# Start-up and one late wait of an AdaLN + FFN kernel: who scales batch b, in which order three engines cast, subtract and shift, and product order over four PSUM banks

## The chip, the cores and the metric

The kernel runs on one core of a Trainium2 chip. The metric is the device time of one execution in microseconds (us). The core has five engines that run side by side and meet at semaphores: TensorE (PE in the profile; its weight loads are PEld), VectorE (DVE), ScalarE (ACT), GpSimd (POOL) and SyncE (SP, which here issues every DMA). The matmul accumulators live in PSUM, eight banks of 128 x 512 f32, written `ps`.

## The reference, cut to what matters

```python
q_emb = relu(q @ W3 + b3)                 # [16, 1024], one row per batch
x1 = (n * v + v_sum) * q_emb[:, None, :]  # v: [16, 512, 1024], v_sum over the 512 tokens
y = relu(x1 @ W2 + b2)                    # first big product
gates = softmax(y @ W_router + b_router)  # 6 experts, the two best kept
out = x + y @ W_base + b_base + (y @ A_s) @ B_s + sum over experts of w_e * (y @ A_r[e]) @ B_r[e]
```

All of it is f32 with 1024 x 1024 weights.

## The kernel before, in words

Data is held transposed, features on the 128 partitions and the 512 tokens of a batch in the free dimension. Batches are taken in eight pairs (a, b). Each big product over a pair is a 2 x 2 block product done with seven block products in place of eight (a Strassen-Winograd scheme): `n` = 0 to 6 in the code, each 512 x 512 times 512 x 512. Quadrants of the input are G11, G21 (batch a, first and second half of the features) and G12, G22 (batch b), four tiles of 128 x 512 each, `k` = 0 to 3. Stage 1 (`pair(i)`, i = 0 to 7, g = i) makes y, stage 2 (`pair2(p)`, g = 8 + p) makes the output.

To keep f32 accuracy, every operand is split in a high part (a rounding copy to the type fp32r: `act_hi`, `w_hi`, `yhi`) and a low part (operand minus high part: `act_lo`, `w_lo`, `buf1_lo`), and every block product is three matmuls (`three`, L1372 to L1374). A group (`group(g, n, j)`) is one output tile: 4 values of k times 3 matmuls of 128 x 512. A product is four groups, 48 matmuls.

Each engine has its order written out by hand:

- ACT: sums of x over tokens (`x_sum`, L570), the scaling that makes x1 (`x_scale`, L578), high parts of activations (`high`, L610) and of y (`y_high`, L629), copies out of PSUM (`copy_p0` L637, `copy_u2` L645, `copy_u4` L653, `c12` L663).
- DVE: low parts of activations (`low`, L923), of weights (`w2_low`, L909) and of y (`y_low`, L1004), differences of quadrants (`t1` L935, `t2` L947, `t3` L956, `t4` L962), sums out of PSUM (`c11`, `c22`, `c21`, L969), and in the first pair weight sums `s12`, `s2` (L1094), `r12` for n = 4 (L1121), `r21` for n = 5 (L1133), and the scaling of G12 for pair 0 (L1097 and L1101, semaphores `late_sum`, `late_mean`, `late_x1`).
- POOL: in the first pair high parts of weights (`w2_high`, L524), `a_hi` and `a_lo` (L540, L542), four subtractions for n = 6 (L556), and for every quadrant the tiny product `shift` = token sum times q (`shift_of`, L519), for which `x_scale` on ACT waits.
- PE: the products in order; `project_y(i, c, j)` after the groups of n = 4, 5, 6 (and of the next n = 0) multiplies tile j of y by the router and adapter weights `a_hi`, `a_lo`. It needs that tile's low part. C11 and C12 are the first-half tiles of y of batch a and b.
- SP: all loads and stores, in one queue.

In pair i, DVE makes the low part of C12 tile 0 before `low(i, 6, 0)`, and those of tiles 1 to 3 inside the loop over `low(i, 6, j)`. `group(0, 0, j)` and `group(0, 1, j)` of the first pair loop over j outside and k inside. Before `group(8, 2, 0)` PE waits for `low_done`, which DVE gives when it has made `low_lo` (L1310).

Of the kernel before, what the change touches and what calls it, by code (L numbers as in the profile page):

```python
# [27 lines left out]
H = 4  # L28
# [9 lines left out]
def adaln_ffn(nc, xT, condT, w3, b3, w2, b2, wbase, bbase, acat, bcat, brouter, outT, E, R):  # L38
# [15 lines left out]
    with ExitStack() as ctx:  # L54
# [119 lines left out]
        w2_hi_done = sem("w2_hi_done")  # L174
        w2_lo_done = sem("w2_lo_done")
# [96 lines left out]
        def source_no(i, q):  # L272

            return (G21, G22).index(q) if i == 0 else 2 + 4 * (i - 1) + (G12, G22, G11, G21).index(q)
# [229 lines left out]
        def _(pool):  # L504
# [38 lines left out]
            for k in range(H):  # L543
                pool.wait_ge(s4_made, H)
                pool.wait_ge(w2_lo_done, 2 * H + k + 1)
                w2_high(4, r12, k)
            for k in range(H):
                pool.wait_ge(s3_made, H)
                w2_high(5, r21, k)
            for k in range(H):  # L550
                pool.wait_ge(w2_lo_done, 4 * H + k + 1)
                w2_high(6, r22, k)
            shift_of(1, G12)
            for k in range(H):
                pool.wait_ge(w2_hi_done, 5 * H + k + 1)
# [10 lines left out]
        def _(act):  # L566
            def x_sum(i, q, k, done=x_summed):
# [3 lines left out]
                                     accum_out=vsum[:, t:t + 1]).then_inc(done, 1)  # L571
# [131 lines left out]
            for k in range(H):  # L703
                x_sum(0, G12, k, late_sum)
# [23 lines left out]
            def pair(i):  # L728
# [160 lines left out]
        def _(dve):  # L889
# [177 lines left out]
            first_w2_low(0)  # L1067
            first_w2_low(1)
# [539 lines left out]
```

## Time and profile before

| | |
|---|---|
| median of 3 runs | 1469.94 us (1467.17 to 1470.19) |
| profiled execution, its own time | 1470.98 us |
| span of the profile | 1469.2 us |
| PE busy | 1434.4 us, 98% |
| DVE busy | 908.0 us, 62% |
| ACT busy | 673.7 us, 46% |
| POOL busy | 48.4 us, 3% |
| mean granted TensorE clock | 0.994 |

The span runs from the first to the last instruction of the profiled execution; the own time is 1.8 us longer and holds what lies around it. Busy time of an engine is not bound to be on the path: what matters is where PE, busy 98% of the span, waits. All times in rows are us from the span's start unless a column says ns.

### The profile page before, as it was taken

Reading aid. Unit: us, or ns where it says so; the run is one execution under the profiler, and the core shown is the slowest. Engines: PE = TensorE matmul, PEld = TensorE weight load, DVE = VectorE, ACT = ScalarE, POOL = GpSimd, SP = SyncE. Lnnn points to the kernel's source line nnn. Section 1 sums busy time; section 2 is a strip of 40 time slices with the busy share of each in tenths; the row PEclk is TensorE's granted clock in tenths of the full one; section 3 lists DMA queues with packets and bytes.
Section 4 is the critical chain, followed back from the end, with each engine's and each line's share of the span. In section 5 each row is a group of like instructions: output and inputs, shape, how many; then the busy total and the mean of one; then the engine's idle time right before and its main releaser. Section 6 shows DMA issues by size and latency. Waiting matters only on the chain.

```text
span 1469.2 us, 18249 instructions
## 1 busy us (share of the span) xinstructions
PE 1434.4 (98%) x6314; PEld 1171.1 (80%) x6314; DVE 908.0 (62%) x1545; ACT 673.7 (46%) x1295; POOL 48.4 (3%) x74
## 2 busy tenths in 40 slices
PE   8879999999999999999999999999999999999999
PEld 4668878788787887878887888888888888888887
DVE  6947566465664656646787856466564655555564
ACT  5565674756748567484543423131232323223230
POOL 3430000000000000000000000000000000000000
PEclk9999999999999999999999999999999999999999
DMA  8231332413324132242562815426172451726342
GB/s 302 78 116 51 119 111 74 134 58 118 105 79 137 53 127 94 80 136 86 208 237 76 283 59 199 166 86 245 65 257 81 165 200 51 273 65 212 132 130 100
DMA packets 107229, 196.30 MB, mean 134 GB/s; under 512 B 12160, under 2 KB 12160, under 8 KB 107136
## 3 DMA queue, kind: packets, MB, share of 16 engines
q1 hardware_dynamic: 107136, 195.13, 39.2%
q8 instruction: 50, 0.82, 0.2%
q14 instruction: 43, 0.35, 0.1%
HBM read 123.78 MB, written 71.30 MB: 133 GB/s over the span
## 4 chain that ended last, share of the span: by engine, by line
PE 90%; DVE 3%; issue 2%; ACT 2%; POOL 1%; DMA 0%; SPq 0%; ACTq 0%; DVEq 0%; POOLq 0%
PE ps L1372 30%; PE ps L1374 29%; PE ps L1373 29%; ACT src L578 1%; POOL w_hi L524 1%; ACT act_hi L610 1%; DVE w_lo L909 1%; DVE act_lo L923 1%; PE ps L1486 0%; DVE buf_lo L1004 0%; DMA src<-in_xT 0%; DVE buf L969 0%; PE ps L1480 0%; ACT src L570 0%; ACT yhi L629 0%
## 5 line engine op out<-in xcount | busy, mean ns | idle before, releaser
L1372 PE MATMUL ps<-act_hi,w_hi 128*128 128x512 f32 x1792 | 703.9, 393 | 9.4 <-DVE act_lo L923 7.6
L1373 PE MATMUL ps<-act_lo,w_hi 128*128 128x512 f32 x1792 | 699.8, 390 | 0.0
L1374 PE MATMUL ps<-act_hi,w_lo 128*128 128x512 f32 x1792 | 699.6, 390 | 0.0
L1372 PEld LDWEIGHTS ps<-act_hi,w_hi 128*128 128x128 f32 x1792 | 337.7, 188 | 81.2 <-issue 7.7
L1374 PEld LDWEIGHTS ps<-act_hi,w_lo 128*128 128x128 f32 x1792 | 337.9, 189 | 71.0
L1373 PEld LDWEIGHTS ps<-act_lo,w_hi 128*128 128x128 f32 x1792 | 338.0, 189 | 69.3
L610 ACT ACTIVATE act_hi<-src 128x512 fp32r<-128x512 f32 x380 | 233.5, 623 | 258.9 <-PE ps L1374 257.2
L923 DVE TENSOR_TENSOR act_lo<-src,act_hi 128x512 fp32r<-128x512 f32 x320 | 218.8, 688 | 154.7 <-ACT act_hi L610 153.7
L969 DVE SCALAR_TENSOR_TENSOR buf<-ps,bb_sb,buf 128x512 f32<-128x512 f32 x128 | 95.7, 749 | 165.2 <-PE ps L1374 148.1
L969 DVE SCALAR_TENSOR_TENSOR buf<-ps,b_sb,buf 128x512 f32<-128x512 f32 x96 | 71.7, 749 | 75.6 <-PE ps L1374 75.2
L629 ACT ACTIVATE yhi<-buf 128x512 fp32r<-128x512 f32 x128 | 80.0, 625 | 52.5 <-PE ps L1374 52.3
L645 ACT ACTIVATE buf<-ps 128x512 f32<-128x512 f32 x64 | 38.3, 598 | 126.7 <-PE ps L1374 126.7
L637 ACT ACTIVATE buf<-ps 128x512 f32<-128x512 f32 x64 | 37.9, 597 | 125.1 <-PE ps L1374 125.1
L578 ACT ACTIVATE src<-src,shift,qn 128x512 f32<-128x512 f32 x120 | 87.7, 803 | 11.7 <-POOL shift L519 11.7
L570 ACT ACTIVATE src<-src 128x512 f32<-128x512 f32 x124 | 76.8, 620 | 0.0
L653 ACT ACTIVATE buf<-ps 128x512 f32<-128x512 f32 x64 | 38.3, 598 | 80.1 <-PE ps L1374 80.1
L923 DVE TENSOR_TENSOR act_lo<-buf,act_hi 128x512 fp32r<-128x512 f32 x64 | 42.6, 687 | 49.6 <-ACT act_hi L610 49.6
L1372 PE MATMUL ps<-yhi,a_hi 128*128 128x512 f32 x128 | 51.1, 399 | 18.5 <-DVE buf_lo L1004 18.0
L920 DVE SCALAR_TENSOR_TENSOR act_lo<-src,act_hi 128x512 fp32r<-128x512 f32 x64 | 44.0, 687 | 34.7 <-ACT act_hi L610 34.7
L1004 DVE TENSOR_TENSOR buf_lo<-buf,yhi 128x512 fp32r<-128x512 f32 x64 | 43.8, 685 | 22.2 <-ACT yhi L629 22.2
L1373 PE MATMUL ps<-buf_lo,a_hi 128*128 128x512 f32 x128 | 50.1, 391 | 0.0
L1374 PE MATMUL ps<-yhi,a_lo 128*128 128x512 f32 x128 | 50.1, 391 | 0.0
(114 smaller groups left out, 1009.4 us busy)
## 6 DMA issues: line engine op xcount, KB each, us to landing
src<-in_xT SPq DMA_DIRECT2D x224, 256.0 KB, 2.8
y_scratch<-buf SPq DMA_DIRECT2D x128, 256.0 KB, 2.1
src<-y_scratch SPq DMA_DIRECT2D x128, 256.0 KB, 4.8
outT<-buf SPq DMA_DIRECT2D x128, 256.0 KB, 4.1
buf<-in_xT SPq DMA_DIRECT2D x32, 256.0 KB, 4.5
wl_raw<-in_wbase SPq DMA_DIRECT2D x6, 1024.0 KB, 6.2
r<-in_w SPq DMA_DIRECT2D x16, 256.0 KB, 8.0
wh_raw<-in_wbase SPq DMA_DIRECT2D x3, 1024.0 KB, 7.7
```

The lines of the kernel that those rows point to most:

```text
L570: nc.scalar.activation(src[:, t, :], src[:, t, :], ACT.Copy, accum_out=vsum[:, t:t + 1]).then_inc(done, 1)
L578: nc.scalar.activation(src[:, t, :], src[:, t, :], ACT.Identity, bias=shift[:, t:t + 1], scale=qn[:, H * HALF_OF[q] + k, 2 * i + BATCH_OF[ ...
L610: nc.scalar.activation(act_hi[:, slot(g, n, k), :], source[:, t, :], func).then_inc(hi_done, 1)
L629: nc.scalar.activation(yhi[:, (y_no(i, c, j) - 1) % 2, :], buf[:, j, :], func).then_inc(yhi_done, 1)
L645: nc.scalar.activation(buf2[:, j, :], ps[:, j, :], ACT.Copy).then_inc(u2_copied, 1)
L920: nc.vector.scalar_tensor_tensor(act_lo[:, s, :], source, 0.0, act_hi[:, s, :].bitcast(F32), ALU.max, ALU.subtract).then_inc(lo_done, 1)
L923: nc.vector.tensor_tensor(act_lo[:, s, :], source, act_hi[:, s, :].bitcast(F32), ALU.subtract).then_inc(lo_done, 1)
L969: nc.vector.scalar_tensor_tensor(buf, ps[:, bank, :], bias, buf, ALU.add, ALU.add).then_inc(done, 1)
L1004: nc.vector.tensor_tensor(lo, y, hi, ALU.subtract).then_inc(ylo_done, 1)
L1372: nc.tensor.matmul(out, wh, a_h, start=start, stop=False, skip_group_check=onto)
L1373: nc.tensor.matmul(out, wh, a_l, start=False, stop=False, skip_group_check=onto)
L1374: return nc.tensor.matmul(out, wl, a_h, start=False, stop=stop, skip_group_check=onto)
```

## The change

Four things are done. (1) In pair 0, batch b's first half (G12) is scaled by ACT (`x_scale(0, G12)`) with a `shift` from POOL, where DVE did it with its own mean; the sources are renumbered. (2) On DVE, ACT and POOL of the first pair, weight and activation parts stand at other places: DVE interleaves `w2_low(2)` with `t1` and `low(0, 2)` with `t2`; POOL makes the high parts of `s12` only after `low(0, 2, 3)`; the high part of the n = 4 weights is cast by ACT in place of POOL; `shift_of(1, G12)` stands ahead of the casts for n = 6. (3) PE does products 0 and 1 of pair 0 with k outside and the four banks inside (`first_groups`). (4) In every pair of stage 1 `y_low(i, C12, 1)` stands ahead of `low(i, 6, 0)`; and PE's wait for `low_done` moves from ahead of `group(8, 2, 0)` to ahead of the low-rank matmuls behind it.

```diff
@@ gpsimd @@
             for k in range(H):
                 pool.wait_ge(s2_made, k + 1)
                 w2_high(2, s2, k)
+                if k == 1:
+                    shift_of(0, G12)
             shift_of(0, G22)
+            pool.wait_ge(q_sum, 1)
+            pool.wait_ge(lo_done, op_no(0, 2, H - 1))
             for k in range(H):
                 pool.wait_ge(s1_made, k + 1)
-                pool.wait_ge(q_sum, 1)
                 w2_high(3, s12, k)
...
             for k in range(H):
-                pool.wait_ge(s4_made, H)
-                pool.wait_ge(w2_lo_done, 2 * H + k + 1)
-                w2_high(4, r12, k)
-            for k in range(H):
                 pool.wait_ge(s3_made, H)
                 w2_high(5, r21, k)
+            shift_of(1, G12)
             for k in range(H):
                 pool.wait_ge(w2_lo_done, 4 * H + k + 1)
                 w2_high(6, r22, k)
-            shift_of(1, G12)
@@ scalar @@
-            for k in range(H):
+            for k in range(H - 1):
                 first_hi(k)
             act.wait_ge(q_sum, 2)
             nc.scalar.activation(qrow[:, D // 2:D], ps[0:NB, Q_BANK + 1, :], ACT.Copy).then_inc(q_copied, 1)
+            first_hi(H - 1)
...
-            x_scale(0, G22)
             for j in range(H):
                 copy_p0(0, j)
+            x_scale(0, G12)
+            x_scale(0, G22)
...
                 if i > 0:
                     exponent(i - 1, GA)
+                else:
+                    for k in range(H):
+                        act.wait_ge(s4_made, H)
+                        act.wait_ge(w2_lo_done, 2 * H + k + 1)
+                        nc.scalar.activation(w_hi[:, 4, k, :], r12[:, k, :], ACT.Copy).then_inc(s4_hi_done, 1)
                 copy_u2(i, H - 1)
@@ vector @@
-            dve.wait_ge(late_sum, H)
-            nc.vector.tensor_scalar(shift[:, cols], vsum[:, cols], 1.0 / T, None, ALU.mult).then_inc(late_mean, 1)
-            dve.wait_ge(late_mean, 1)
-            for k in range(H):
-                t = tile(G12, k)
-                nc.vector.tensor_scalar(src[:, t, :], src[:, t, :], shift[:, t:t + 1], qn[:, k, 1:2],
-                                        ALU.add, ALU.mult).then_inc(late_x1, 1)
+            w2_low(2, s2, (0, 1))
             for k in range(H):
                 t1(0, k)
-            w2_low(2, s2)
+                if k >= 2:
+                    w2_low(2, s2, (k,))
             for k in range(H):
                 t2(0, k)
+                if k > 0:
+                    low(0, 2, k - 1)
+            low(0, 2, H - 1)
...
                 y_low(i, C12, 0)
+                y_low(i, C12, 1)
                 for j in range(H):
                     low(i, 6, j)
                     if j > 0:
                         c22(i, j - 1)
+                    if j >= 2:
                         y_low(i, C12, j)
@@ tensor @@
+            def first_groups(n):
+                for k in range(H):
+                    pe.wait_ge(lo_done, op_no(0, n, k))
+                    pe.wait_ge(w2_lo_done, H * n + k + 1)
+                    for j in range(H):
...
+                    if k == 0 and n == 0:
+                        turn(1)
...
             def low_rank_c11(p, j):
                 if j == 0:
+                    if p == 0:
+                        pe.wait_ge(low_done, 1)
                     pe.wait_ge(lr_lo_done, 3 * p + 1)
...
-                if p == 0:
-                    pe.wait_ge(low_done, 1)
```

On DVE, before, between the sum `s2` and the end of the n = 4 weight difference of the first pair (`src<-src` is `t1`, `buf<-src` is `t2`):

```order
L1094 TENSOR_TENSOR s<-s,r 128x512 x4
L1097 TENSOR_SCALAR shift<-vsum 128x4
L1101 TENSOR_SCALAR src<-src,shift,qn 128x512 x4
L935 TENSOR_TENSOR src<-src 128x512 x4
L909 TENSOR_TENSOR w_lo<-s,w_hi 128x512 x4
L947 TENSOR_TENSOR buf<-src 128x512 x4
L923 TENSOR_TENSOR act_lo<-buf,act_hi 128x512 x4
L969 SCALAR_TENSOR_TENSOR buf<-ps,b_sb,buf 128x512 x4
L909 TENSOR_TENSOR w_lo<-s,w_hi 128x512 x4
L1121 TENSOR_TENSOR r<-r,s 128x512 x4
```

The same stretch of DVE in the changed kernel, whose line numbers differ:

```order
L1101 TENSOR_TENSOR s<-s,r 128x512 x4
L916 TENSOR_TENSOR w_lo<-s,w_hi 128x512 x2
L941 TENSOR_TENSOR src<-src 128x512 x3
L916 TENSOR_TENSOR w_lo<-s,w_hi 128x512
...
L953 TENSOR_TENSOR buf<-src 128x512
L930 TENSOR_TENSOR act_lo<-buf,act_hi 128x512
L953 TENSOR_TENSOR buf<-src 128x512
L930 TENSOR_TENSOR act_lo<-buf,act_hi 128x512 x2
L975 SCALAR_TENSOR_TENSOR buf<-ps,b_sb,buf 128x512 x4
L916 TENSOR_TENSOR w_lo<-s,w_hi 128x512 x4
L1123 TENSOR_TENSOR r<-r,s 128x512 x4
```

The five scaling instructions are gone, and low parts stand between the differences; from `c11` (`buf<-ps,b_sb,buf`) on the order is as it was.

On POOL, before, from the casts of `s2` (n = 2) on, with the semaphores waited for:

```order
L524 CAST w_hi<-s 128x512 [waits s2_made] x4
L519 TENSOR_TENSOR shift<-vsum,q 128x4 [waits x_summed]
L524 CAST w_hi<-s 128x512 [waits q_sum,s1_made] x4
L540 CAST a_hi<-a_raw 128x1024 [waits a_loaded]
L542 TENSOR_TENSOR a_lo<-a_raw,a_hi 128x1024 [waits a_hi_made]
L524 CAST w_hi<-r 128x512 [waits w2_lo_done,s4_made] x4
L524 CAST w_hi<-r 128x512 [waits s3_made] x4
L524 CAST w_hi<-r 128x512 [waits w2_lo_done] x4
L519 TENSOR_TENSOR shift<-vsum,q 128x4 [waits x_summed]
```

And in the changed kernel:

```order
L522 CAST w_hi<-s 128x512 [waits s2_made] x2
L517 TENSOR_TENSOR shift<-vsum,q 128x4 [waits x_summed]
L522 CAST w_hi<-s 128x512 [waits s2_made] x2
L517 TENSOR_TENSOR shift<-vsum,q 128x4 [waits x_summed]
L522 CAST w_hi<-s 128x512 [waits s1_made,lo_done,q_sum]
L522 CAST w_hi<-s 128x512 [waits s1_made] x3
L541 CAST a_hi<-a_raw 128x1024 [waits a_loaded]
L543 TENSOR_TENSOR a_lo<-a_raw,a_hi 128x1024 [waits a_hi_made]
L522 CAST w_hi<-r 128x512 [waits s3_made] x4
L517 TENSOR_TENSOR shift<-vsum,q 128x4 [waits x_summed]
L522 CAST w_hi<-r 128x512 [waits w2_lo_done] x4
```

The casts of `s12` and the two `a` instructions now wait for `lo_done`, the four n = 4 casts are gone, and the last `shift` shown, that of (1, G12), has four casts less ahead of it.

## Rows read from the trace of the kernel before

**Rows 1.** The page, its first line.

```profile
span 1469.2 us, 18249 instructions
```

**Rows 2.** Waits of PE, whole span: us in total, times, longest us.

```profile
PE ps L1372 <- DVE buf_lo L1004: 18.0, 8, 6.0
PE ps L1372 <- DVE act_lo L923: 7.6, 2, 7.0
```

**Rows 3.** Timeline of PE: start, us, instruction, idle before and its releaser.

```profile
40.67 0.39 PE L1374 MATMUL ps<-act_hi,w_lo 128*128 128x512 f32 x1
48.05 0.77 PE L1372 MATMUL ps<-act_hi,w_hi 128*128 128x512 f32 x1 [6.99 <-DVE act_lo L923]
...
53.10 0.40 PE L1372 MATMUL ps<-act_hi,w_hi 128*128 128x512 f32 x1
...
61.27 0.39 PE L1372 MATMUL ps<-act_hi,w_hi 128*128 128x512 f32 x1
...
87.80 0.80 PE L1372 MATMUL ps<-yhi,a_hi 128*128 128x512 f32 x1 [5.96 <-DVE buf_lo L1004]
...
285.13 0.50 PE L1372 MATMUL ps<-yhi,a_hi 128*128 128x512 f32 x1 [1.73 <-DVE buf_lo L1004]
...
788.69 0.50 PE L1372 MATMUL ps<-act_hi,w_hi 128*128 128x512 f32 x1 [1.71 <-DVE low_lo L1310]
```

**Rows 4.** Windows: busy PE, PEld, DVE, ACT, POOL, then granted clock, DMA.

```profile
87.00:93.00 6.00, 5.21 (x12) 4.13 (x13) 3.51 (x6) 5.01 (x12) 0.20 (x1) 0.50 0.71 201
...
100.00:104.00 4.00, 2.29 (x10) 1.58 (x9) 3.56 (x7) 3.69 (x11) 0.00 (x0) 1.00 0.54 158
...
790.00:793.00 3.00, 3.00 (x9) 2.37 (x8) 3.00 (x6) 0.53 (x2) 0.00 (x0) 0.52 0.26 93
```

**Rows 5.** Timeline of DVE, first pair, up to product 2.

```profile
35.80 4.57 DVE L935 TENSOR_TENSOR src<-src 128x512 f32<-128x512 f32 x4
40.29 4.64 DVE L909 TENSOR_TENSOR w_lo<-s,w_hi 128x512 fp32r<-128x512 f32 x4
...
49.68 2.71 DVE L969 SCALAR_TENSOR_TENSOR buf<-ps,b_sb,buf 128x512 f32<-128x512 f32 x4
```

**Rows 6.** Timeline of DVE, first pair, low parts alone and beside POOL's casts.

```profile
57.13 2.48 DVE L923 TENSOR_TENSOR act_lo<-src,act_hi 128x512 fp32r<-128x512 f32 x4
...
75.37 4.11 DVE L909 TENSOR_TENSOR w_lo<-r,w_hi 128x512 fp32r<-128x512 f32 x4 [0.71 <-POOL w_hi L524]
```

**Rows 7.** Timeline of POOL, first pair.

```profile
38.33 1.50 POOL L540 CAST a_hi<-a_raw 128x1024 fp32r<-128x1024 f32 x1
39.90 2.68 POOL L542 TENSOR_TENSOR a_lo<-a_raw,a_hi 128x1024 fp32r<-128x1024 f32 x1
...
57.27 7.64 POOL L524 CAST w_hi<-r 128x512 fp32r<-128x512 f32 x1 [14.69 <-DVE r L1121]
...
74.72 6.35 POOL L524 CAST w_hi<-r 128x512 fp32r<-128x512 f32 x8 [7.23 <-DVE r L1133]
```

**Rows 8.** Timeline of ACT, first pair: scalings, and high part of C11 tile 2.

```profile
35.08 2.94 ACT L578 ACTIVATE src<-src,shift,qn 128x512 f32<-128x512 f32 x4 [2.09 <-POOL shift L519]
...
81.27 2.93 ACT L578 ACTIVATE src<-src,shift,qn 128x512 f32<-128x512 f32 x4 [8.32 <-POOL shift L519]
...
86.33 0.62 ACT L629 ACTIVATE yhi<-buf 128x512 fp32r<-128x512 f32 x1
```

**Rows 9.** A later pair: high part of C12 tile 1 (ACT), its store (SP).

```profile
277.99 0.62 ACT L629 ACTIVATE yhi<-buf 128x512 fp32r<-128x512 f32 x1
...
272.14 0.44 SPq L391 DMA_DIRECT2D y_scratch<-buf  x1
```

**Rows 10.** Timeline of DVE at the start of stage 2.

```profile
788.55 0.68 DVE L1240 TENSOR_TENSOR ha_lo<-ha_raw,ha_hi 128x512 fp32r<-128x512 f32 x1
...
796.11 0.68 DVE L1259 TENSOR_TENSOR buf<-ps,buf 128x512 f32<-128x512 f32 x1
```

**Rows 11.** The page, DMA issues: KB each, us to landing.

```profile
y_scratch<-buf SPq DMA_DIRECT2D x128, 256.0 KB, 2.1
```

More of the change, by code:

```diff
@@ L272, in source_no @@
         def source_no(i, q):
-            return (G21, G22).index(q) if i == 0 else 2 + 4 * (i - 1) + (G12, G22, G11, G21).index(q)
+            return (G21, G12, G22).index(q) if i == 0 else 3 + 4 * (i - 1) + (G12, G22, G11, G21).index(q)
         def tile_no(i, q, k):
@@ L566, in _, with x_sum @@
         def _(act):
-            def x_sum(i, q, k, done=x_summed):
+            def x_sum(i, q, k):
                 t = tile(q, k)
@@ L570, in x_sum @@
                 nc.scalar.activation(src[:, t, :], src[:, t, :], ACT.Copy,
-                                     accum_out=vsum[:, t:t + 1]).then_inc(done, 1)
+                                     accum_out=vsum[:, t:t + 1]).then_inc(x_summed, 1)
             def x_scale(i, q):
@@ L904, in first_w2_low, with w2_low @@
                                         ALU.subtract).then_inc(w2_lo_done, 1)
-            def w2_low(n, raw):
-                for k in range(H):
-                    dve.wait_ge(w2_hi_done, H * (n - 1) + k + 1)
+            def w2_low(n, raw, ks=range(H)):
+                for k in ks:
+                    if n == 4:
+                        dve.wait_ge(s4_hi_done, k + 1)
+                    else:
+                        dve.wait_ge(w2_hi_done, H * (1, 2, 3, 5).index(n) + k + 1)
                     nc.vector.tensor_tensor(w_lo[:, n, k, :], raw[:, k, :], w_hi[:, n, k, :].bitcast(F32),
@@ L1067, in _ @@
             first_w2_low(0)
+            condition(0)
             first_w2_low(1)
@@ L1083, in _ @@
             low(0, 0, 3)
+            w2_low(1, r12, (0,))
             condition(1)
-            w2_low(1, r12)
+            w2_low(1, r12, (1, 2, 3))
             for k in range(H):
@@ L1112, in first_pair @@
             def first_pair():
-                for j in range(H):
-                    low(0, 2, j)
                 for j in range(H):
@@ L1458, in group @@
                 mm.then_inc(bank_done, 1)
+            def first_groups(n):
[3 more added lines that the diff above has]
+                    for j in range(H):
+                        if k == 0:
+                            bank_free(0, n, j)
+                        cols = slice(j * P, (j + 1) * P)
+                        mm = three(ps[:, j if n == 0 else Z_BANK + j, :], w_hi[:, n, k, cols], w_lo[:, n, k, cols],
+                                   act_hi[:, slot(0, n, k), :], act_lo[:, slot(0, n, k), :], k == 0, k == H - 1)
+                        if k == H - 1:
+                            mm.then_inc(bank_done, 1)
+                    if k < H - 1:
+                        mm.then_inc(op_used, 1)
+                    if k == 0 and n == 0:
+                        turn(1)
             def project_y(i, c, j):
@@ L1489, in pair @@
             def pair(i):
-                for j in range(H):
-                    group(i, 0, j)
-                    if i > 0:
+                if i == 0:
+                    first_groups(0)
+                    first_groups(1)
+                else:
+                    for j in range(H):
+                        group(i, 0, j)
                         project_y(i - 1, C21, j)
@@ L1495, in pair @@
                             turn_h(i - 1, GB)
-                    elif j == 0:
-                        turn(1)
-                for j in range(H):
-                    group(i, 1, j)
-                    if j == 1 and i > 0:
-                        turn_gates(i - 1, GB)
+                    for j in range(H):
+                        group(i, 1, j)
+                        if j == 1:
+                            turn_gates(i - 1, GB)
                 for j in range(H):
```

20 lines of the change are left out of this document (7 added, 13 removed).

## The prediction, made blind

> **What bounds the kernel now.** The page's first line gives the span [rows 1]; the table before it says PE is busy for 98% of it. So the first view is who PE waits for [rows 2]: the low part of y on DVE (`buf_lo`, 18.0 us in 8 waits) and the low part of an activation (`act_lo`, 7.6 us). The timeline of PE places them [rows 3]. PE stands 6.99 us between products 1 and 2 of the first pair (until 48.05), 5.96 us in product 4 of the first pair ahead of `project_y(0, C11, 2)` (until 87.80), and 1.73 us in a later pair ahead of `project_y(i, C12, 1)` (285.13). The `buf_lo` total less 5.96 leaves 12.0 us in 7 such waits, one for each of the pairs 0 to 6. At the start of stage 2 it stands 1.71 us for `low_lo` (788.69). The rest is matmuls: 36 of them start between 53.10 and 61.27 [rows 3], 0.227 us each, so a product of 48 is 10.9 us and a `project_y` 0.7 us.
>
> Idle time also cost clock. From 87 to 93 the granted clock was 0.50, that is 1.2 in place of 2.4 GHz [rows 4], although PE was at work from 87.80: with the half us behind that window, about 3.0 us lost. The 12 matmuls from 48.05 to 53.10 took 5.05 in place of 2.7 us [rows 3], 2.3 lost. From 790 to 793 it was 0.52 [rows 4] after an idle of only 1.71 us, about 1.7 lost with the end of the stretch. After the like idle at about 101 it was 1.00 [rows 4].
>
> **The change, step by step.** My sum follows the DVE-ACT-POOL chain of the first pair, because PE waits for it.
>
> *Product 2 starts earlier.* Now ACT is free at 33.0 (35.08 less its wait of 2.09) and scales only G22 [rows 8]. In the new order four copies from PSUM come first (each about 0.5, an estimate by the pitch of 0.62 us instructions [rows 8]), less something under 1 us because the second half of q is turned after 12 matmuls of product 0 instead of after the whole first group with its wait. I take 34.2. Then eight scalings at 0.71 [rows 8] end at 39.9. DVE loses its scalings and finds its `t1` and `w2_low(2)` without a full port fight: they take 4.57 and 4.64 us for four now [rows 5] where four subtractions alone take 2.48 [rows 6]. Its first `low(0, 2)` then ends near 41, and with one `t2` and one `low` in turn (0.6 each) the last near 44.2; `c11` starts there and not at 49.68 [rows 5], 5.5 earlier. Product 1 now ends with the matmul at 40.67 [rows 3]; with k outside, products 0 and 1 no longer wait in between and end 1.4 earlier. PE then waits about 1.7 us, runs product 2 haltingly at first, and ends it near 53.2, 8 earlier than 61.27.
>
> *DVE up to the n = 5 weights.* Behind 44.2 DVE has the same work as before: 4 `c11` (2.64 by their pitch [rows 5]) and 34 subtractions at 0.60 [rows 6] up to the last `s3` (L1133), 20.5: end at 67.3 if nothing disturbs it. But the casts of `s12`, `a_hi` and `a_lo`, which POOL did at 35 to 42.6, now fall here, since the POOL order waits for `low(0, 2, 3)`. Their price: nothing at the least. At the most: POOL gets in only when DVE stops for the first cast (as the cast at 57.27, 7.64 us long [rows 7]), 0.5; three `w2_low(3)` beside casts at 1.03 and not 0.60 [rows 6], 1.3; one beside `a_hi`, 1.50 long, 0.9 more; one behind `a_lo`, 2.68 long [rows 7], 2.2 more; together 4.9. `a_lo` and `a_hi` are priced by their own rows, the casts may in part pass beside `c11`; I take 4.0. So `s3` ends at 71.3, where POOL now starts its casts at 74.72 [rows 7]. `low(0, 3, 0)` comes at about 56.2, so PE gets a new wait of some 3 us ahead of product 3 (53.2 to 56.2); the 8 us gained are back to 5.
>
> The Trainium skill, GPSIMD Engine Reference, Specifications, says that GpSimd contends for SBUF with those VectorE instructions that have two SBUF inputs or run in a two-port mode. `c11` has one input in PSUM, so by that rule the `s12` casts would be done beside `c11`, the price would be nearer 3.1 than 4.0, and the forecast 1447.1. No row here has POOL at work beside an L969.
>
> *The n = 4 casts on ACT* cost ACT four instructions of 0.6 [rows 8] and put its `copy_u2(0, 3)`, `high(0, 4, j)` and the sums of the next pair behind `s4_made`. They end near 58, and DVE asks for `low(0, 4, 0)` only near 65: hidden. POOL loses its 7.64 us cast; nobody waited long for it.
>
> *The shift of (1, G12).* Now it comes behind 8 casts, 6.35 us [rows 7], and ACT waits for it 8.32 us, to 81.27 [rows 8]; from there it is 6.5 us to the matmul at 87.80 [rows 3] through `y_high(0, C11, 2)` at 86.33 [rows 8]. With four casts ahead of it: 71.3 + 3.2 + 0.2 = 74.7, then 6.5, then 0.3 for POOL's remaining casts and subtractions, which now fall beside DVE's `y_low`: 81.6. That is 6.2 earlier than 87.80. PE has come there at 56.2 + 10.9 + 9.5 = 76.6, so it still stands 5.0 us. Clock: the idle of 5.96 cost 3.0, idles of 1.7 cost 0 and 1.7; for 5.0 I take 2.5, a gain of 0.5. The bounds are 0 and 3.0.
>
> *`y_low(i, C12, 1)`.* In a later pair its high part is there at 277.99 + 0.62 [rows 9], and the store of its buffer was issued at 272.14 [rows 9] and lands about 2.1 us later [rows 11]. DVE can make it at 278.7 to 279.4; PE asks for it at 285.13 - 1.73 = 283.4 [rows 3]. All seven waits go: 12.0. Behind it on DVE stands `low(i, 6, 0)`, whose high part comes later still, so nothing is held up. What is late next on PE: nothing within 4 us.
>
> *`low_done`.* PE goes on 1.71 us earlier; `low_rank_c11(0, 0)` then comes one group (2.7) after 788.69 - 1.71 = 787.0, at 789.7, and its `ha_lo` is ready at 788.55 + 0.68 = 789.2 [rows 10]. With the idle goes its clock loss of 1.7. The add of the low-rank part at 796.11 [rows 10] may hold the third of these groups by a few tenths: 3.2.
>
> Sum: 6.2 + 0.5 + 12.0 + 3.2 = 21.9. The profiled execution took 1470.98 (span 1469.2), so 1449.1; it lies 1.04 above the median of 1469.94, and I forecast the median: 1448.0.
>
> **Rivals.**
>
> 1. *The port costs little or the clock stays up.* Casts beside `c11`, `a_lo` starved and done in a pause: contention nearly 0 gives 4.0 more, a kept clock 2.5 more. For it: casts of four took POOL only 3.2 [rows 7]. Against it: four subtractions beside `a_lo` took 4.64 [rows 5] and not 2.48 [rows 6], and `y_high` needs it. 1441.5; both halves seldom together, 1444 is its middle.
> 2. *The first pair gains nothing.* The moved POOL work, cold clock and ACT's stop at `s4_made` add up to 6.7 on the chain, for example if a starved `a_lo` (as the cast at 57.27 [rows 7]) stops ACT at `y_high(0, C11, 0)` and with it `high(0, 4, 3)`, about 4 us, on top of 4.0. Then 12.0 + 3.2 alone are left: 1454.7.
> 3. *The waits move on, the kernel doesn't get faster.* PE would stop at the next `project_y` or at product 6 in each pair. `c22` and `y_high(i, C12, 2)` depend on PE's own groups and move with it; I see nothing. 1463 (first pair and stage 2 alone, less 3).
> 4. *Slower.* `y_low(i, C12, 1)` also waits for the store of its buffer, and now stands ahead of the `low(i, 6, j)`. If stores landed late, DVE would stand with all of product 6 behind it. It decides from where the landing costs PE more than 1.73 in each of 7 pairs plus the other 9.9 / 7 = 1.4, so from 283.4 - 0.7 + 3.1 = 285.8, 13.7 us after issue at 272.14, against 2.1 in [rows 11]. At 15 us: 1479.
>
> **How the numbers follow.** My case 0.62, rival 1 0.20, rival 2 0.12, rival 3 0.03, rival 4 0.02, no change at all 0.01. What a measurement of this kernel can tell from no change is 0.2%, 2.9 us. Faster: 0.97. The range for 8 in 10 takes in my case with its bounds, 1444.5 to 1452, and most of rivals 1 and 2: 1442 to 1455.
>
> **What would show it.** Right: PE's waits have no `buf_lo` of 1.7 in pairs 0 to 6; the wait ahead of product 2 is under 2.5; a wait of 1 to 4 us stands ahead of product 3 and one of 3 to 5.5 ahead of `project_y(0, C11, 2)`, which starts at 80 to 83; `low_lo` is gone from the waits, and the clock near 790 is 1.00. Wrong: `c11` of pair 0 later than 46, ACT's `y_high(0, C11, 0)` waiting for `a_lo`, or a new PE wait of over 1 us that comes again in each pair.

## The result, and the profile after

| | before | changed |
|---|---|---|
| median | 1470.07 us (4 runs, 1467.17 to 1470.79) | 1448.88 us (4 runs, 1448.59 to 1449.11) |
| ratio | | 0.9859, 95% interval 0.9842 to 0.9877 |
| profiled execution, its own time | 1470.98 us | 1448.76 us |
| mean granted TensorE clock | 0.994 | 0.996 |

The changed kernel is 21.2 us faster by the medians and 22.2 by the two profiled executions (the one of the kernel before lies 0.9 above its median); 1448.0 was forecast. The page of the changed kernel, its first line and its first busy row, beside [rows 1]:

```profile
span 1446.7 us, 18245 instructions
...
PE 1429.2 (99%) x6314; PEld 1168.9 (81%) x6314; DVE 905.4 (63%) x1540; ACT 677.9 (47%) x1303; POOL 39.7 (3%) x71
```

PE is busy 5.2 us less than before in a span that is 22.5 us shorter: most of what went was idle time. Its waits, whole span, where [rows 2] had 18.0 us in 8 and 7.6 us in 2:

```profile
PE ps L1376 <- DVE buf_lo L1010: 6.0, 1, 6.0
PE ps L1376 <- issue: 4.2, 2, 3.0
```

One wait for `buf_lo` of this kind is left, 6.0 us long; the seven of 1.73 are gone, and so is the one for `low_lo`. The `act_lo` row is gone too, but two waits of 4.2 us in all stand under "issue" (a wait for nothing that the profile shows). The timeline of PE places all three, against [rows 3]:

```profile
39.24 0.39 PE L1378 MATMUL ps<-act_hi,w_lo 128*128 128x512 f32 x1
...
42.63 0.47 PE L1376 MATMUL ps<-act_hi,w_hi 128*128 128x512 f32 x1 [2.99 <-issue]
...
56.79 0.47 PE L1376 MATMUL ps<-act_hi,w_hi 128*128 128x512 f32 x1 [1.24 <-issue]
...
83.49 0.79 PE L1376 MATMUL ps<-yhi,a_hi 128*128 128x512 f32 x1 [6.01 <-DVE buf_lo L1010]
...
87.50 0.39 PE L1376 MATMUL ps<-act_hi,w_hi 128*128 128x512 f32 x1
```

PE stops after the matmul of 39.24, which ends product 1, and product 2 starts at 42.63; product 3 starts at 56.79, and `project_y(0, C11, 2)` at 83.49, 4.31 earlier than the 87.80 of [rows 3]. Whom the two "issue" waits were for is told by the timeline of DVE:

```profile
41.83 0.69 DVE L930 TENSOR_TENSOR act_lo<-buf,act_hi 128x512 fp32r<-128x512 f32 x1 [0.34 <-ACT act_hi L607]
...
45.64 2.72 DVE L975 SCALAR_TENSOR_TENSOR buf<-ps,b_sb,buf 128x512 f32<-128x512 f32 x4
...
48.27 5.41 DVE L916 TENSOR_TENSOR w_lo<-s,w_hi 128x512 fp32r<-128x512 f32 x4
...
56.01 2.48 DVE L930 TENSOR_TENSOR act_lo<-src,act_hi 128x512 fp32r<-128x512 f32 x4
...
81.68 1.75 DVE L1010 TENSOR_TENSOR buf_lo<-buf,yhi 128x512 fp32r<-128x512 f32 x1
```

The `low` at 41.83 ends at 42.52 and PE starts at 42.63; the first of the four at 56.01 ends 0.69 later, at 56.70, and PE starts at 56.79. Both waits are for low parts of an activation. `c11` (L975) starts at 45.64, not at 49.68 [rows 5]. And the `y_low` (L1010) that PE waits for at 83.49 took 1.75 us, where one alone takes 0.69. POOL says why:

```profile
45.84 2.29 POOL L522 CAST w_hi<-s 128x512 fp32r<-128x512 f32 x4 [10.56 <-issue]
48.08 1.04 POOL L541 CAST a_hi<-a_raw 128x1024 fp32r<-128x1024 f32 x1
49.20 2.72 POOL L543 TENSOR_TENSOR a_lo<-a_raw,a_hi 128x1024 fp32r<-128x1024 f32 x1
71.81 3.20 POOL L522 CAST w_hi<-r 128x512 fp32r<-128x512 f32 x4 [19.88 <-DVE r L1135]
74.97 0.64 POOL L517 TENSOR_TENSOR shift<-vsum,q 128x4 f32<-128x4 f32 x1
...
78.27 6.31 POOL L553 TENSOR_TENSOR w_lo<-r,w_hi 128x512 fp32r<-128x512 f32 x4
```

The casts of `s12` (45.84), `a_hi` and `a_lo` lie behind product 2's low parts, as the new order wants. The casts for n = 5 start at 71.81 and not at 74.72 [rows 7], and the shift of (1, G12) is done at 75.61. From 78.27 the four subtractions for n = 6 (L553) run, and `y_low` at 81.68 falls among them. ACT, beside [rows 8]:

```profile
30.94 0.63 ACT L567 ACTIVATE src<-src 128x512 f32<-128x512 f32 x1 [1.10 <-DMA src<-in_xT]
...
35.52 5.76 ACT L575 ACTIVATE src<-src,shift,qn 128x512 f32<-128x512 f32 x8
...
75.64 2.93 ACT L575 ACTIVATE src<-src,shift,qn 128x512 f32<-128x512 f32 x4 [7.05 <-POOL shift L517]
...
80.70 0.62 ACT L626 ACTIVATE yhi<-buf 128x512 fp32r<-128x512 f32 x1
```

ACT waited 1.10 us for a load of x at 30.94, began to scale G12 at 35.52, and scaled (1, G12) from 75.64, 5.63 earlier than 81.27 in [rows 8]. The high part of C11 tile 2 (80.70) is ready at 81.32. The granted clock, beside [rows 4]:

```profile
83.50:86.50 3.00, 3.00 (x7) 2.42 (x8) 2.83 (x3) 2.42 (x8) 1.08 (x1) 0.50 0.49 159
767.00:770.00 3.00, 3.00 (x16) 2.40 (x16) 2.64 (x5) 0.00 (x0) 0.00 (x0) 1.00 0.00 0
```

Behind the wait of 6.01 it is 0.50, as before; the stretch is shorter. The nine matmuls from 83.49 to 87.50 took 4.01 us, and 2.04 at the 0.227 of full clock: 1.97 lost. In the kernel before, the 14 matmuls from 87.80 to 93.89 (the first at full pitch again) took 6.09 in place of 3.18: 2.9 lost, behind a wait of the same length (5.96). At the start of stage 2 (767 to 770) the clock is 1.00.

**Where the time came from.** I subtract the start of the same matmul in one trace from that in the other, place by place. Product 2 starts 5.42 earlier, product 3 4.49 earlier, `project_y(0, C11, 2)` 4.31 earlier, and the matmuls behind both slow stretches of product 4 (from 93.89 before, 88.65 now) 5.24 earlier. Each of the pairs 0 to 6 then adds 2.01 to 2.06, 14.2 together. The start of stage 2 adds 3.1: 1.8 of wait and 1.6 of clock, less 0.3 that is given back further on, at 777.43, where PE now waits for DVE's add of the low-rank part. 5.2 + 14.2 + 3.1 = 22.5, the difference of the spans.

Of the 5.2, the last 0.9 is clock, and no run shows that the change made it: the wait in product 4 did not get shorter (6.01 and 5.96). Experiments 1 and 2 below keep the first pair of the kernel before, wait 5.74 and 5.59 there, and lose 1.6 and 1.7 behind it where the kernel before lost 2.9. The window of experiment 2 that stands beside the first of [rows 4], where the clock was 0.50:

```profile
87.00:93.00 6.00, 5.03 (x15) 4.05 (x16) 3.69 (x6) 5.17 (x13) 0.20 (x1) 0.64 0.74 208
```

So what the slow clock costs behind this wait differs by over 1 us between traces of the same first pair, and the first pair's gain is known no better than that: 4.3 at the start of `project_y(0, C11, 2)`, 5.2 behind it.

### The profile page after: what moved, and what is told of

Same layout as the page of the kernel before. It is cut to its first block, busy times and chain, and to the rows that moved or that the text cites. A ratio compares the mean times of both kernels' runs of the same rounds, so it can differ in the third digit from the quotient of the medians.

```text
span 1446.7 us, 18245 instructions
## 1 busy us (share of the span) xinstructions
PE 1429.2 (99%) x6314; PEld 1168.9 (81%) x6314; DVE 905.4 (63%) x1540; ACT 677.9 (47%) x1303; POOL 39.7 (3%) x71
## 4 chain that ended last, share of the span: by engine, by line
PE 93%; DVE 3%; ACT 1%; issue 0%; POOL 0%; DVEq 0%; ACTq 0%
PE ps L1376 31%; PE ps L1378 31%; PE ps L1377 31%; DVE act_lo L930 1%; PE ps L1508 0%; DVE w_lo L916 0%; ACT src L575 0%; PE ps L1502 0%; DVE buf L975 0%; DVE src L962 0%; POOL w_hi L522 0%; DVE buf_lo L1010 0%; DVE wl_raw L1153 0%; DVE r L1135 0%; DVE src L968 0%
## 5 line engine op out<-in xcount | busy, mean ns | idle before, releaser
L975 DVE SCALAR_TENSOR_TENSOR buf<-ps,bb_sb,buf 128x512 f32<-128x512 f32 x128 | 95.7, 749 | 164.7 <-PE ps L1378 149.3
L975 DVE SCALAR_TENSOR_TENSOR buf<-ps,b_sb,buf 128x512 f32<-128x512 f32 x96 | 71.7, 749 | 66.2 <-PE ps L1378 65.8
L1010 DVE TENSOR_TENSOR buf_lo<-buf,yhi 128x512 fp32r<-128x512 f32 x64 | 44.9, 703 | 38.7 <-ACT yhi L626 38.7
```

Of the source, the lines that this page charges most:

```text
L975: nc.vector.scalar_tensor_tensor(buf, ps[:, bank, :], bias, buf, ALU.add, ALU.add).then_inc(done, 1)
L1010: nc.vector.tensor_tensor(lo, y, hi, ALU.subtract).then_inc(ylo_done, 1)
```

## The experiments

Each kernel was timed beside the kernel before, on the same chip. "Before" below is that median. The intervals of the ratios are about 2 us wide to either side. The changed kernel was not timed again beside experiments 4 to 10, which ran on other occasions; the medians of the kernel before moved from 1470.07 to between 1470.44 and 1470.69, so a difference from the changed kernel of under 1 us says nothing by the times alone. What such a difference is made of is read from the traces.

**1. Only `y_low(i, C12, 1)` moved.**

```diff
                 y_low(i, C12, 0)
+                y_low(i, C12, 1)
                 for j in range(H):
                     low(i, 6, j)
                     if j > 0:
                         c22(i, j - 1)
+                    if j >= 2:
                         y_low(i, C12, j)
```

> The kernel before with one edit alone: the low part of C12 tile 1 ahead of low(i, 6, 0) in every pair. Theory A: each of the seven waits is worth more than the idle that the waits' view names, because the matmuls behind it start 0.1 apart from their pitch and the end of the last one is modelled; by the shift between the two traces 2.05 us each, 14.4 in all, so 1455.7 us, ratio 0.990. Theory B, as the prediction had it: 1.73 each, 12.0 in all, 1458.1, ratio 0.992. If the waits only moved on: ratio 1.000.

Measured: 1456.01 us against 1470.44, ratio 0.9903 (0.9890 to 0.9917), 14.4 less. Its waits of PE:

```profile
PE ps L1374 <- DVE act_lo L923: 7.7, 2, 7.0
PE ps L1374 <- DVE buf_lo L1004: 5.7, 1, 5.7
...
PE ps L1374 <- DVE low_lo L1312: 1.7, 1, 1.7
```

Seven waits of 1.73 are gone, and nothing took their place: the three that stay are those of [rows 2] and [rows 3] that this edit doesn't touch. The interval of the ratio (12.2 to 16.2 us) holds 14.4 and just excludes 12.1; the trace is sharper: from behind product 4 of the first pair to the start of stage 2 it gains 14.2 on the kernel before. The idle column understates the stall. In the kernel before, around the wait of 285.13 in [rows 3]:

```profile
283.01 0.39 PE L1374 MATMUL ps<-act_hi,w_lo 128*128 128x512 f32 x1
...
285.47 0.39 PE L1373 MATMUL ps<-buf_lo,a_hi 128*128 128x512 f32 x1
```

From 283.01 to 285.13 are 2.12 us, where one matmul of the stream takes 0.227: 1.89 lost, though the column says 1.73, because it counts from the modelled end (0.39 after the start). The first matmul behind the wait takes 0.34 to the next, 0.11 more than in the stream. That makes 2.0 for each, and 14.0 for seven, 0.2 short of the 14.2; the next few matmuls, each up to 0.02 slower, hold the rest.

**2. Only the wait for `low_done` moved.**

```diff
+                    if p == 0:
+                        pe.wait_ge(low_done, 1)
                     pe.wait_ge(lr_lo_done, 3 * p + 1)
...
-                if p == 0:
-                    pe.wait_ge(low_done, 1)
                 for j in range(H):
```

> The kernel before with one edit alone: PE waits for low_done only ahead of the low-rank matmuls. Theory A: the idle of 1.71 us and the low clock behind it both go, 3.3 us, ratio 0.9978, and the granted clock near 790 us is 1.00. Theory B: the clock falls there for another reason than the idle; then 1.9 us, ratio 0.9987, and the clock still falls.

Measured: 1467.13 against 1470.44, ratio 0.9980 (0.9971 to 0.9989), 3.3 less. Its waits, and the window in which [rows 4] had a clock of 0.52:

```profile
PE ps L1372 <- DVE buf_lo L1004: 17.7, 8, 5.6
```

```profile
790.00:793.00 3.00, 3.00 (x15) 2.46 (x14) 2.90 (x8) 1.16 (x3) 0.00 (x0) 1.00 0.56 149
```

The eight waits for `buf_lo` stay, the one for `low_lo` is gone, and the clock is 1.00. The time alone (1.6 to 4.3 us by its interval) would not exclude theory B's 1.9; the clock does. In the trace the start of stage 2 gains 3.4 on the kernel before, 1.8 of stall and 1.6 of slow clock that it brought, and 0.3 of it is given back at the third low-rank group.

**3. Only the first pair changed** (parts 1, 2 and 3 of the change; parts of (4) as before).

```diff
                 y_low(i, C12, 0)
-                y_low(i, C12, 1)
                 for j in range(H):
...
-                    if j >= 2:
                         y_low(i, C12, j)
...
-                    if p == 0:
-                        pe.wait_ge(low_done, 1)
                     pe.wait_ge(lr_lo_done, 3 * p + 1)
...
+                if p == 0:
+                    pe.wait_ge(low_done, 1)
```

The diff is against the changed kernel.

> The changed kernel with the low part of C12 tile 1 and the wait for low_done put back to their old places, so that only the start-up of pair 0 is changed. Theory A: the start-up is worth what the two traces differ by before the first C12 wait, 4.9 us, ratio 0.9967. Theory B, as the prediction had it: 6.7 us, ratio 0.9954. Either way the seven waits of 1.7 us are back.

Measured: 1465.58 against 1470.44, ratio 0.9967 (0.9955 to 0.9980), 4.9 less.

```profile
PE ps L1374 <- DVE buf_lo L1010: 18.1, 8, 6.0
PE ps L1374 <- issue: 3.4, 2, 2.6
PE ps L1374 <- DVE low_lo L1312: 1.7, 1, 1.7
```

The first pair's waits are those of the changed kernel (the two "issue" waits 0.8 shorter), all the others those of before. By the times the three parts sum to 14.4 + 3.3 + 4.9 = 22.6, where the whole change measured 21.2, each with an interval of some 2 us. The traces say it more closely: from this kernel to the changed one the seven places give 14.1 and the start of stage 2 3.0, against 14.2 and 3.1 with the first pair unchanged. None hides another.

**4. The shift of (1, G12) ahead of the n = 5 casts too.** From here on each diff is against the changed kernel.

```diff
             nc.gpsimd.tensor_tensor(a_lo[:], a_raw[:], a_hi[:].bitcast(F32), ALU.subtract).then_inc(a_made, 1)
+            shift_of(1, G12)
             for k in range(H):
                 pool.wait_ge(s3_made, H)
                 w2_high(5, r21, k)
-            shift_of(1, G12)
```

> The changed kernel with one more edit: on POOL the shift of (1, G12) ahead of the four casts for n = 5 as well. Theory A: PE's 6.0 us wait in product 4 of pair 0 is set by the chain last weight difference, four casts, shift, ACT's scaling; with the shift free at once ACT scales at about 68.6 in place of 75.6 us, and the wait falls to under 2.5 us, its clock loss with it: 4 to 6 us under the changed kernel, 1443 to 1445. Theory B: DVE sets it (the low parts of the n = 5 weights stand ahead of the low part of y): the wait falls by 1 to 2 us only, 1447.

Measured: 1445.03, ratio 0.9829 (0.9816 to 0.9842), 3.9 under the changed kernel. PE's wait in product 4 is 2.19 and not 6.01. But the shift, 128 x 4 values, took POOL 4.72 us (first row), while DVE ran subtractions end to end, the last of them the `s3` of 69.73 (second row), which ends at 72.23, 0.06 before the shift does:

```profile
67.56 4.72 POOL L517 TENSOR_TENSOR shift<-vsum,q 128x4 f32<-128x4 f32 x1 [15.16 <-ACT src L567]
```

```profile
69.73 2.50 DVE L1135 TENSOR_TENSOR r<-r 128x512 f32<-128x512 f32 x4
...
79.01 1.09 DVE L1010 TENSOR_TENSOR buf_lo<-buf,yhi 128x512 fp32r<-128x512 f32 x1
```

A shift takes POOL 0.20 when DVE is quiet. Here POOL got in when DVE stopped. It is not so once POOL is at work. Its eight casts behind the shift follow each other without a break, and DVE's low parts beside them, just as unbroken, take turns with them one for one, some 1.07 and 1.09 each:

```profile
72.29 7.27 POOL L522 CAST w_hi<-r 128x512 fp32r<-128x512 f32 x8
```

```profile
76.97 2.11 DVE L930 TENSOR_TENSOR act_lo<-src,act_hi 128x512 fp32r<-128x512 f32 x2
```

ACT scaled from 72.32, and not from 68.6 as theory A had it; behind it the low part of C11 tile 2 (79.01) is again the last to come, now because DVE itself is busy up to it with instructions of 1.09 beside POOL's casts.

**5. POOL's subtractions for n = 6 wait until C11's low parts are made.**

```diff
                 pool.wait_ge(w2_hi_done, 4 * H + k + 1)
+                pool.wait_ge(ylo_done, y_no(0, C11, 3))
                 nc.gpsimd.tensor_tensor(w_lo[:, 6, k, :], r22[:, k, :], w_hi[:, 6, k, :].bitcast(F32),
```

> The changed kernel with one more edit: POOL's four subtractions for the n = 6 weights wait until the low part of C11 tile 3 of pair 0 is made. Theory A: they hold DVE's low parts there (1.50 and 1.75 us in place of 0.68), and the last of these is what PE waits for; then the wait of 6.0 us falls by 1.1 to 1.5 us, 1447.5. Theory B: the length of DVE's instructions there comes from something else; no change, 1448.9.

Measured: 1448.78, ratio 0.9851 (0.9836 to 0.9866), no different from the changed kernel. DVE and PE:

```profile
81.48 0.69 DVE L1011 TENSOR_TENSOR buf_lo<-buf,yhi 128x512 fp32r<-128x512 f32 x1 [0.47 <-ACT yhi L627]
```

```profile
82.23 0.79 PE L1377 MATMUL ps<-yhi,a_hi 128*128 128x512 f32 x1 [3.11 <-DVE buf_lo L1011]
...
99.03 0.50 PE L1377 MATMUL ps<-yhi,a_hi 128*128 128x512 f32 x1 [1.33 <-DVE buf_lo L1011]
```

The cause was as supposed: with POOL out of the way the low part of C11 tile 2 takes 0.69 in place of 1.75, and `project_y(0, C11, 2)` starts at 82.23, 1.26 earlier than 83.49. (The wait is 3.11 and not 6.01 also because PE comes 1.6 later: in this execution it waited 1.90 ahead of product 3, and its clock fell to half behind that.) All of the gain is lost at 99.03, in a wait of 1.33 ahead of `project_y(0, C12, 2)`, 16.8 us on; in the changed kernel PE comes there at 99.10 with nothing to wait for (the low part is ready at 98.79). It hangs on ACT's scaling of (1, G22), which this edit did not make earlier: the shift for it stands behind the delayed subtractions.

**6. POOL without the wait for `low(0, 2, 3)`**: the casts of `s12`, `a_hi` and `a_lo` fall where they did before.

```diff
             pool.wait_ge(q_sum, 1)
-            pool.wait_ge(lo_done, op_no(0, 2, H - 1))
             for k in range(H):
```

> The changed kernel without POOL's new wait for low(0, 2, 3): the s12 casts, a_hi and a_lo follow the shift of (0, G22) at once, near 35 us. Theory A: they hold the same DVE for as long, only earlier, so c11 of pair 0 comes 2 to 3 us later than 45.6, the 2.9 us of contention behind it are gone, and the end is within 1 us of 1448.9; PE's wait ahead of product 2 grows from 3.0 to 5 to 6 us, the one ahead of product 3 goes. Theory B: DVE has slack at 35 to 41 us where it waits for ACT, so the work is free there and the end is 2 to 3 us earlier.

Measured: 1450.02, ratio 0.9861 (0.9847 to 0.9876), 1.1 over the changed kernel. DVE, then POOL, then PE at the start of product 2:

```profile
40.81 2.84 DVE L915 TENSOR_TENSOR w_lo<-s,w_hi 128x512 fp32r<-128x512 f32 x1
...
50.00 2.72 DVE L974 SCALAR_TENSOR_TENSOR buf<-ps,b_sb,buf 128x512 f32<-128x512 f32 x4
```

```profile
40.42 2.67 POOL L542 TENSOR_TENSOR a_lo<-a_raw,a_hi 128x1024 fp32r<-128x1024 f32 x1
```

```profile
46.99 0.77 PE L1375 MATMUL ps<-act_hi,w_hi 128*128 128x512 f32 x1 [6.41 <-issue]
```

One `w2_low(2)` takes 2.84 beside an `a_lo` of 2.67, `c11` starts at 50.00 and not at 45.64, and PE stands 6.41 ahead of product 2. Of these 4.4, 1.2 were there before the moved work: ACT began to scale G12 at 36.69 and not at 35.52, after a wait of 1.41 for a load of x. Nothing waits ahead of product 3 in this run and DVE meets no `a_lo` later, so `project_y(0, C11, 2)` comes only 1.4 later, which is little more than the 1.2: what the move of the POOL work gains is paid back at 48 to 52, all but a few tenths. The intervals of the two ratios overlap, and the spans, 1449.0 and 1446.7, do not settle it either: 0.9 of their 2.3 is a longer slow stretch of clock behind a shorter wait (5.0 us, 2.9 lost). Whether the move is worth anything is not shown.

**7. Products 0 and 1 of the first pair by tile, as before**, but product 1 over four banks, where the kernel before used two.

```diff
-                bank = j if n != 1 else Z_BANK + j % 2
+                bank = j if n != 1 else Z_BANK + (j % 2 if g > 0 else j)
...
                 if i == 0:
-                    first_groups(0)
-                    first_groups(1)
+                    for n in (0, 1):
+                        for j in range(H):
+                            group(0, n, j)
+                            if n == 0 and j == 0:
+                                turn(1)
```

> The changed kernel with products 0 and 1 of pair 0 by output tile again, as before, two groups in turn over all k. Theory A: the 1.3 us that the order by k saves PE lies ahead of a wait for DVE, and only the earlier turn of q feeds the chain; 0 to 1 us slower, 1449.4, the wait ahead of product 2 falls by about 1 us. Theory B: the order by k is what brings the start-up's gain; 1.5 to 3 us slower.

Measured: 1449.18, ratio 0.9854 (0.9840 to 0.9869): no difference that can be told. The wait in product 4 is 6.02 long, as in the changed kernel. By tile PE waits 1.86 ahead of product 2, over the banks 2.99, but not because the order over the banks ends product 1 sooner: its last matmul starts at 39.43 here and at 39.24 there, and the 0.2 are there before product 0 begins. The order over k saves nothing; the wait of 0.66 inside product 0 of the kernel before is gone in both. What differs is the operand. In this execution ACT had no wait for a load of x and began to scale G12 0.95 sooner than at 35.52:

```profile
34.57 5.76 ACT L575 ACTIVATE src<-src,shift,qn 128x512 f32<-128x512 f32 x8
```

Product 2 starts 0.96 sooner, and so does `project_y(0, C11, 2)`, at 82.53; a longer slow stretch behind it takes half of that back. So DVE and ACT decide when product 2 begins, and the landing of a load moves it by up to 1 us between executions. The bank order is worth nothing here.

**8. 24 matmuls put into the wait of product 4.** They are extra work into a bank that is not in use there; no result depends on them.

```diff
                     group(i, 4, j)
+                    if i == 0 and j == 2:
+                        for _ in range(24):
+                            nc.tensor.matmul(ps[:, Z_BANK, :], w_hi[:, 4, 0, 0:P], act_hi[:, slot(0, 4, 0), :],
+                                             start=True, stop=True)
                     project_y(i, C11, j)
```

> The changed kernel with 24 more matmuls in PE's wait of 6.0 us ahead of project_y(0, C11, 2), about 5.4 us of them, into a bank that is free there; their product is not used. Theory A: the low clock from 83.5 to 86.6 us comes from PE's idle time; it goes, and 1.7 us with it, 1447.2. Theory B: it comes with the work that follows, or the matmuls disturb DVE; no change or slower.

Measured: 1447.17, ratio 0.9842 (0.9825 to 0.9858), 1.7 under the changed kernel. PE, and the window behind the wait:

```profile
83.33 0.50 PE L1376 MATMUL ps<-yhi,a_hi 128*128 128x512 f32 x1 [0.64 <-DVE buf_lo L1010]
```

```profile
83.30:86.30 3.00, 2.96 (x13) 2.47 (x14) 2.89 (x3) 2.94 (x8) 1.59 (x2) 1.00 0.53 167
```

`project_y` starts at 83.33, as it did, and the clock behind it is 1.00. So 1.7 us of the changed kernel's time is the slow clock behind the wait, apart from the wait itself, and it can be had back without any operand coming earlier. The two intervals overlap, so the size rests on the trace: there the 2.0 that were lost behind the wait are gone.

**9. As 4, and DVE waits for that shift before `y_low(0, C11, 0)`.**

```diff
+            shift_of(1, G12)
             for k in range(H):
                 pool.wait_ge(s3_made, H)
                 w2_high(5, r21, k)
-            shift_of(1, G12)
...
                     low(0, 4, j)
+                dve.wait_ge(shift_made, source_no(1, G12) + 1)
                 y_low(0, C11, 0)
```

> The kernel of e4_shift_first with one more edit: DVE waits for that shift ahead of the low part of C11 tile 0 of pair 0, so that its chain of back-to-back subtractions has one pause. Theory A: in e4 the shift, 4 columns wide, took 4.72 us because POOL got no access while DVE ran on; with the pause it takes under 0.7 us, ends near 68.7 and ACT scales 3.6 us earlier than in e4. PE's wait ahead of project_y(0, C11, 2) is then set by DVE's order (its low part stands behind eight other instructions), so the time is that of e4 within 1 us, 1445. Theory B: the shift waits for something else and stays over 3 us long.

Measured: 1444.93, ratio 0.9825 (0.9811 to 0.9838). POOL and DVE:

```profile
67.49 1.13 POOL L517 TENSOR_TENSOR shift<-vsum,q 128x4 f32<-128x4 f32 x1 [15.14 <-ACT src L567]
```

```profile
68.65 1.29 DVE L1010 TENSOR_TENSOR buf_lo<-buf,yhi 128x512 fp32r<-128x512 f32 x2
```

With a pause of 0.09 us in DVE's stream the shift takes 1.13 and not 4.72: it ends at 68.62, 0.06 behind the last `low` ahead of the pause. Theory A had said under 0.7; the shift had started at 67.49 and waited for the pause. So it was DVE's unbroken row of two-input instructions that kept POOL out in experiment 4, not the shift's own length. The time is the same as in 4 (0.1 less), because DVE, not ACT, had become last there.

**10. The pieces together**: 9; in pair 0 `y_low(0, C11, 2)` ahead of `low(0, 5, 0)`; and the shift of (1, G22) ahead of POOL's subtractions.

```diff
                 w2_high(6, r22, k)
+            shift_of(1, G22)
             for k in range(H):
...
-            shift_of(1, G22)
...
+                if i == 0:
+                    y_low(0, C11, 2)
                 for j in range(H):
                     low(i, 5, j)
-                    if j in (1, 2):
+                    if j in (1, 2) and (i > 0 or j == 2):
                         y_low(i, C11, j + 1)
```

> The kernel of e9_shift_first_pause with three more edits: in pair 0 the low part of C11 tile 2 ahead of low(0, 5, 0), and on POOL the shift of (1, G22) ahead of the subtractions for n = 6. Theory A: with the shift early and the low part of y early PE waits for it under 1.5 us and keeps its clock there: 2 to 3 us under e4, 1442.5. Theory B: as in e5, what is won at this wait is given back at the next waits of pair 0, since DVE runs without a gap: within 1 us of e4, 1445.

Measured: 1442.50 against 1470.64, ratio 0.9810 (0.9797 to 0.9824): 6.4 under the changed kernel and 28.1 under the kernel before, the fastest of all. PE's waits for `buf_lo` of this kind, `project_y(0, C11, 2)` on PE, POOL's shift, and DVE:

```profile
PE ps L1379 <- DVE buf_lo L1010: 0.8, 1, 0.8
```

```profile
78.88 0.39 PE L1379 MATMUL ps<-yhi,a_hi 128*128 128x512 f32 x1
```

```profile
68.64 0.20 POOL L517 TENSOR_TENSOR shift<-vsum,q 128x4 f32<-128x4 f32 x1 [16.76 <-ACT src L567]
```

```profile
68.88 1.29 DVE L1010 TENSOR_TENSOR buf_lo<-buf,yhi 128x512 fp32r<-128x512 f32 x2 [0.79 <-POOL shift L517]
...
84.66 3.50 DVE L1010 TENSOR_TENSOR buf_lo<-buf,yhi 128x512 fp32r<-128x512 f32 x2 [2.40 <-DMA y_scratch<-buf]
```

`project_y(0, C11, 2)` starts at 78.88 without a wait. With a pause of 0.79 on DVE the shift takes 0.20. One wait of 0.77 is left, at the next place: the two `y_low` of C12 at 84.66 take 3.50 beside POOL's subtractions, and the first of them is what PE waits for. The profile puts DVE's idle ahead of it down to the store of that buffer: the mechanism of rival 4, but its high part is ready only at 84.45, so the store costs 0.2 at the most.

## Why the prediction was right

The sign, the time and the mechanism held; 1448.0 was forecast, 1448.88 measured. Two of its signs did not: the wait ahead of product 2 was to be under 2.5 and was 2.99, and the one ahead of `project_y(0, C11, 2)` was to be 3 to 5.5 with a start at 80 to 83, and was 6.01 with a start at 83.49. By its own steps, forecast and found:

- *Product 2 starts earlier* (`c11` at 44.2; found 45.64). ACT was to scale G12 from 34.2 and began at 35.52. 1.10 of it is a wait for a load of x, which the sum had left out: it took the time at which ACT had been free before (33.0) as free of loads. It is the step that failed most, and the reason why the wait ahead of product 2 was 2.99 and not "under 2.5": in experiment 7, where that wait for a load is missing, ACT began at 34.57 and PE waited 1.86.
- *Contention behind it, 4.0* (found 2.9). Start to start of what DVE did from 45.64 to 53.60: 7.96 for four `c11` and four subtractions, where 2.64 + 2.40 = 5.04 was their price alone: 2.9. The casts of `s12` (2.29 for four) ran beside `c11` (2.72 for four, 2.71 in [rows 5]) and neither was slowed. The Trainium skill, GPSIMD Engine Reference, Specifications, has GpSimd contend only with VectorE instructions with two SBUF inputs or in a two-port mode; the trace agrees, and the price by that rule, 3.1, was nearer than mine. 1.4 late less 1.1 saved: `s3` ended at 71.7, 71.3 was forecast.
- *Product 3*: a wait of some 3 us until 56.2; found 1.24 until 56.79. PE had come there later, by the late start of product 2 and its slow matmuls.
- *The n = 4 casts on ACT, hidden*: ACT stood 2.65 us for them at 56.12, and nobody waited for that.
- *The shift, 3.4 us behind `s3`* (found 3.9, 71.74 to 75.61): the first cast came 0.07 later, and the shift took 0.64 and not 0.2.
- *From the shift to PE, 6.8* (found 7.9). This is the other half of the miss. I had put 0.3 for POOL's subtractions beside DVE's `y_low`; they made that one instruction 1.06 longer (1.75 and 0.69), as experiment 5 shows. In all 83.49 in place of 81.6: 4.3 and not 6.2.
- *Clock, 0.5 gained* (found 0.9: 4.31 at the start of `project_y`, 5.24 behind the slow stretch). The loss at product 4 was taken as 2.5, since the wait was to be shorter; it was 1.97 by the timeline behind a wait that was not shorter. This term came out by luck: the same wait costs 1.6 to 2.9 from one execution to the next.
- *The seven waits, 12.0* (found 14.2 in the trace, 14.4 by the times of experiment 1). The mechanism held; the term was mis-sized, since I took the idle column for the stall.
- *`low_done`, 3.2* (found 3.1 in the trace, 3.3 by the times of experiment 2). The add that "may hold the third of these groups" did: PE waits for it at 777.43, 0.3 net.

So 21.9 was made of 6.7 + 12.0 + 3.2, and the traces gave 5.2 + 14.2 + 3.1 = 22.5: 1.5 too much for the first pair, 2.2 too little for the seven waits. Without the clock's 0.9, which is not the change's, the first pair gave 4.3, and the two errors are over 2 us each with opposite signs. The forecast is closer than its terms deserve. Of the rivals, none came about: the wait in product 4 and its slow clock stayed (against rival 1), the first pair alone gave 4.9 by the times (against 2), experiment 1 gave all that its waits held (against 3), and DVE has no wait for a store of y in the whole trace (against 4).

What stays open: why 1.71 us of idle took the clock down at 788.69 and the 1.71 that ends at 102.81 did not [rows 4]. It is no accident of one execution: all three traces that have the wait at the start of stage 2 (before, experiments 1 and 3) lose 1.6 behind it, and none of the waits of 1.7 ahead of `project_y` loses any. One difference that the traces show is that PE does four short transposes between its last matmul (786.25) and the wait at 788.69, while the others follow a matmul directly; no run took them away.

## What to carry to other kernels

Size a stall by start to start over the gap, less what the stream would have taken, and not by the idle column: here 2.03 stood behind each 1.73. When a wait is removed, look how far behind it the next operand is ready: in experiment 5 a gain of 1.26 was lost 16.8 us later to an operand that had been just in time. When VectorE runs two-input instructions end to end, a GpSimd instruction on which a third engine waits and which comes up in the midst of them needs a pause placed for it, however small it is; one that directly follows another GpSimd instruction got its turn here without one (the shift behind four casts took 0.64). And before a gain of 1 us is believed, look at what the same stretch does in the traces of kernels in which it was not changed: here a load and the clock moved it by as much.

## What was not expected of the hardware

- GpSimd was kept out by a VectorE that never stopped, for a 128 x 4 instruction of 0.20: 4.72 us in experiment 4. A pause of 0.09 us let it in (1.13 in all, experiment 9), one of 0.79 made it 0.20 (experiment 10). The Trainium skill, SBUF — State Buffer, SBUF: two separate sides, says that of a VectorE instruction with two SBUF inputs and a GpSimd one that reads SBUF, the one that starts first gets the shared pair of ports for the whole instruction and the other blocks. The runs agree for one instruction against one (the 2.84 beside an `a_lo` of 2.67, experiment 6), and show besides that a GpSimd instruction that comes up while VectorE runs without a pause does not get its turn between two of them: seven started while the shift waited, and eleven while the cast at 57.27 did that took 7.64 [rows 7]. GpSimd instructions that directly follow another did get it, one for one (experiment 4, from 72.9).
- Casts on GpSimd and `c11`, which has one input in PSUM, ran side by side at full speed: 2.29 for four and 2.72 for four.
- The length of an idle did not tell whether the clock fell, nor for how long: 1.24 (ahead of product 3) and seven of 1.7 cost nothing, 1.71 at the start of stage 2 cost 1.6, 1.90 ahead of product 3 in experiment 5 1.6, and the wait of some 6 us in product 4 from 1.6 to 2.9.
